# A graph-network kernel: where the fused node pieces stand in the last attention groups

## The reference, cut to what matters

```python
ft = (hn @ W_att).reshape(n, H, DH)            # H = 10 heads of DH = 13: 130 numbers a node
scores = einsum('ehd,ehd->eh', ft[src], ft[dst]) / sqrt(DH)
ex = exp(scores - segment_max(scores, dst)[dst])
a = ex / segment_sum(ex, dst)[dst]
agg = segment_sum(ft[src] * a[:, :, None], dst)
out = elu(agg).reshape(n, H * DH) @ hr_w + hr_b + hn
out = layer_norm(out); skip2 = out
out = elu(elu(out @ w1 + b1) @ w2 + b2) + skip2
x = x + out; h = relu(layer_norm(x))           # the second block's input
```

## Time and profile before

| | |
|---|---|
| median of 3 runs | 3837.37 us (3832.4 to 3840.59) |
| the profiled execution | 3839.02 us, its span 3837.3 us |
| TensorE busy | 3360.4 us (88%) |
| VectorE busy | 2355.0 us (61%) |
| ScalarE busy | 1781.7 us (46%) |
| GpSimd busy | 2447.0 us (64%) |
| mean granted clock of TensorE | 0.889 of full speed |

### The profile page before, as it was taken

One profiled execution on the slowest core, in us unless ns is written; L12 is line 12 of the kernel. 1 busy time (PEld: TensorE's weight loads), 2 busy tenths in 40 slices (PEclk: granted clock), 3 DMA queues, 4 the chain that ended last, 5 costly groups with the idle time before them and its releaser, 6 DMA issues. The chain is left out here.

```text
span 3837.3 us, 59210 instructions
## 1 busy us (share of the span) xinstructions
PE 3360.4 (88%) x20346; PEld 2104.3 (55%) x20346; DVE 2355.0 (61%) x3511; ACT 1781.7 (46%) x4855; POOL 2447.0 (64%) x2604
## 2 busy tenths in 40 slices
PE   5788888888888888888878487999999999999999
PEld 4566666666666666666655354444444444445444
DVE  8798888888888888888655375222422242224222
ACT  4787887878888888788543255000200020002000
POOL 2577777777777777777765000777277737764775
PEclk7688888888888888888888698999999999999999
DMA  6433333334333333334322514888788868887886
GB/s 205 127 105 107 107 104 106 103 107 108 103 107 104 107 107 104 107 103 128 89 56 50 109 36 128 256 256 257 218 256 256 256 211 254 253 246 219 262 262 189
DMA packets 493480, 600.98 MB, mean 157 GB/s; under 512 B 61561, under 2 KB 424420, under 8 KB 492910
## 3 DMA queue, kind: packets, MB, share of 16 engines
q1 hardware_dynamic: 355270, 337.43, 29.2%
q0 software_dynamic: 82960, 172.57, 18.2%
q10 hardware_dynamic: 54968, 87.43, 6.4%
HBM read 489.80 MB, written 109.00 MB: 156 GB/s over the span
## 5 line engine op out<-in xcount | busy, mean ns | idle before, releaser
L984 POOL DMA_INDIRECT fts<-ft_tab,src_all x1568 | 1480.7, 944 | 504.2 <-issue 473.4
L2668 PE MATMUL cv_acc<-cv_cnt,cv_parts 128*128 128x512 bf16 x5880 | 1271.9, 379 | 0.0
L2668 PEld LDWEIGHTS cv_acc<-cv_cnt,cv_parts 128*128 128x128 bf16 x5880 | 575.3, 98 | 690.8
L2419 POOL DMA_INDIRECT cv_slots<-hs_tab,slot_idx x640 | 605.0, 945 | 195.0 <-issue 195.0
L1016 DVE TENSOR_TENSOR ohk<-iota_ps,key_cols 128x784 bf16<-128x784 f32 x704 | 651.3, 967 | 5.5
L1432 PE MATMUL agg_ps<-terms,oh 128*64 128x141 f32 x2744 | 566.4, 382 | 82.8 <-DVE terms L1053 82.2
L1432 PEld LDWEIGHTS agg_ps<-terms,oh 128*64 128x64 f32 x2744 | 492.0, 192 | 131.3 <-DVE terms L1053 116.4
L1193 ACT ACTIVATE dist_l<-lo_iota,low 128x128 bf16<-128x128 f16 x1760 | 533.1, 387 | 16.5 <-ACT low L1188 0.4
L1372 PE MATMUL adj_ps<-ohk,ohl 128*128 128x196 bf16 x2816 | 379.4, 262 | 93.5 <-ACT strip L1245 48.0
L1245 ACT CAST strip<-adj_ps 128x392 bf16<-128x392 f32 x704 | 334.2, 475 | 238.8 <-PE adj_ps L1375 205.0
L1030 DVE TENSOR_TENSOR prod<-ftd_ps,fts 128x780 f32<-128x780 f32 (+1 forms) x392 | 271.1, 691 | 242.0 <-DMA fts<-ft_tab,src_all 208.4
(11 more groups left out here) (345 smaller groups left out, 3455.0 us busy)
## 6 DMA issues: line engine op xcount, KB each, us to landing
cv_cnt<-adj SPq DMA_DIRECT2D x88, 2048.0 KB, 8.3
cv_cnt<-adj SPq DMA_DIRECT2D x44, 2176.0 KB
adj<-strip ACTq DMA_DIRECT2D x176, 392.0 KB
fts<-ft_tab,src_all POOLq DMA_INDIRECT x1568
win<-ft_tab SPq DMA_DIRECT2D x196, 65.0 KB
hs_tab<-cv_hs ACTq DMA_DIRECT2D x24, 448.0 KB, 3.6
cv_slots<-hs_tab,slot_idx POOLq DMA_INDIRECT x640
agg_tab<-res SPq DMA_DIRECT2D x196, 35.2 KB
```

Source lines behind the costliest of these rows:

```text
L984: nc.gpsimd.indirect_dma_start(fts[u][:, k, :], None, ft_tab[:, :], bass.IndirectOffsetOnAxis(src_all[:, n, k:k + 1], 0)).then_inc(gathere ...
L2419: nc.gpsimd.indirect_dma_start(slots[n % RING][:, e, :], None, hs_tab[:, :], bass.IndirectOffsetOnAxis(rows_at, 0)).then_inc(slots_in[n % ...
L2668: last = nc.tensor.matmul(a[:, 0:width], parts[:, r, b, :], cnt[q][:, 0:width // SUB, (b - b0) * SUB:(b - b0 + 1) * SUB], start=(b == 0 an ...
```

## The change

Five things change, in `attention` alone. `STARTS` goes from (0, 5, 17, 22) to (0, 5, 15, 20), and `SLOTS_AT` from 177 to 176: units 0 and 1 begin one group earlier, units 2 and 3 two groups earlier. GpSimd's wait for `shift_done` stands in counted groups only. VectorE puts weighted and fade_boundary at the start of a step without counts. ScalarE puts `res` ahead of the first half's pieces. TensorE has an order of its own for steps without counts: nearness, first half's pieces, closeness, the sums, last_features, the last sum, first_features, second half's pieces. No instruction is added or taken away on the three compute engines.

```diff
--- before.py
+++ after.py
@@ -86,7 +86,7 @@
 FT = FB * BATCH
 UNITS = ((0, 4), (4, 4), (8, 3), (11, 3))
 UW = 4
-STARTS = (0, 5, 17, 22)
+STARTS = (0, 5, 15, 20)
 PHASES = 17
 FINAL_AT = 130
 CQ = ((0, 393), (393, 392), (785, 392), (1177, 392))
@@ -782,7 +782,7 @@
     x_sb, eps, hnT_dram, hT_tab = (g[k] for k in ("x_sb", "eps", "hnT_dram", "hT_tab"))
     R3 = HD + 1 - P
     WEIGHTS_AT = 2 * UN
-    SLOTS_AT = NSD + 1
+    SLOTS_AT = NSD
     NODES_AT = NSD - 8
     LD = 6
     FU = 6
@@ -978,7 +978,7 @@
                 if n >= FU:
                     pool.wait_ge(terms_done, n - FU + 1)
                 for k in range(GC):
-                    if k == HC and n >= LAG + 1:
+                    if k == HC and LAG + 1 <= n < NSD:
 
                         pool.wait_ge(shift_done, n - LAG)
                     nc.gpsimd.indirect_dma_start(fts[u][:, k, :], None, ft_tab[:, :],
@@ -1153,23 +1153,27 @@
 
             def body(k):
                 one, two, late = k.at(-1), k.at(-2), k.at(-LAG)
+                def weights():
+                    weighted(late)
+                    if late.after(1):
+                        fade_boundary(late)
                 if k.counted():
                     low_one_hots(k)
                     key_one_hots(k, 0)
                     key_one_hots(k, 1)
                     key_one_hots(k, 2)
+                elif late.exists():
+                    weights()
                 if one.exists():
                     first_products(one)
                 if two.exists():
                     highest(two)
                 if k.counted():
                     key_one_hots(k, 3)
+                    if late.exists():
+                        weights()
                 for unit, phase in units_at(k, 0):
                     nodes(unit, phase)
-                if late.exists():
-                    weighted(late)
-                    if late.after(1):
-                        fade_boundary(late)
                 if one.exists():
                     last_products(one)
                 for unit, phase in units_at(k, 1):
@@ -1329,12 +1333,12 @@
                     numerators(late)
                 if nxt.exists():
                     destination_rows(nxt)
-                for unit, phase in units_at(k, 0):
-                    nodes(unit, phase)
                 if k.counted():
                     copy_quarter(k, 1)
                 if over.exists():
                     result(over)
+                for unit, phase in units_at(k, 0):
+                    nodes(unit, phase)
                 if nxt.exists():
                     destination_columns(nxt)
                 for unit, phase in units_at(k, 1):
@@ -1530,32 +1534,49 @@
                     broadcast_highest(late)
                 if two.exists():
                     turn_highest(two)
-                for unit, phase in units_at(k, 0):
-                    nodes(unit, phase)
-                if k.counted():
-                    count(k, 0)
-                if nxt.exists():
-                    nearness(nxt)
-                if k.counted():
-                    count(k, 1)
-                    count(k, 2)
-                if one.exists():
-                    last_features(one)
-                if nxt.exists():
-                    closeness(nxt)
-                for unit, phase in units_at(k, 1):
-                    nodes(unit, phase)
-                if k.counted():
-                    count(k, 3)
-                if late.exists():
-                    first_sums(late)
-                    later_sums(late)
-                if k.exists():
-                    first_features(k)
-                if late.exists():
+                def last_sums():
                     if late.after(1):
                         carried(late)
                     last_sum(late)
+
+                def counted():
+                    count(k, 0)
+                    if nxt.exists():
+                        nearness(nxt)
+                    count(k, 1)
+                    count(k, 2)
+                    if one.exists():
+                        last_features(one)
+                    if nxt.exists():
+                        closeness(nxt)
+                    count(k, 3)
+                    if late.exists():
+                        first_sums(late)
+                        later_sums(late)
+                    first_features(k)
+                    if late.exists():
+                        last_sums()
+
+                def uncounted():
+                    if nxt.exists():
+                        nearness(nxt)
+                    for unit, phase in units_at(k, 0):
+                        nodes(unit, phase)
+                    if nxt.exists():
+                        closeness(nxt)
+                    first_sums(late)
+                    later_sums(late)
+                    if one.exists():
+                        last_features(one)
+                    last_sums()
+                    if k.exists():
+                        first_features(k)
+                    for unit, phase in units_at(k, 1):
+                        nodes(unit, phase)
+                if k.counted():
+                    counted()
+                else:
+                    uncounted()
             zero = Group(0)
             nearness(zero)
             closeness(zero)
```

## The result

The changed kernel takes 3801.81 us (median of 4 runs, 3794.61 to 3807.49), the kernel before 3836.02 us beside it. The ratio is 0.9909, with a 95% interval from 0.9885 to 0.9933: 34 us faster (26 to 44). The profiled execution of the changed kernel took 3796.92 us; it is one of the two quick ones of the four.

What follows compares the result with a forecast made beforehand. Gathers were taken to bound the counted steps, then TensorE's work plus waits. Gains of 16 (waits), 3 (earlier units), 2 (clock) and 0 (GpSimd) made 21 us: 3837.4 to 3816.4 us, own range 3808 to 3825, eight in ten 3802 to 3833.

Steps and rivals of the forecast that it cites:

- TensorE's clock: Steps 179 to 194: granted clock rises from 0.82 to 0.84 as waits shrink, worth 3 us, taken as 2.
- What bounds the kernel: Attention stage: GpSimd's gathers at 9.99 us a group up to 1905 us, then TensorE's work plus waits between its pieces.
- GpSimd's wait: Groups 176 to 195: removing 29.5 us of shift waits gains 0, since GpSimd is ahead of the other engines.
- The waits of TensorE: Steps 179 to 194: the new order cuts TensorE's 40.0 us of waits to 24 us, 16 us won.
- eight crossings: Second half's piece to the next step's first: TensorE waits 1.0 us for the elu each time, 8 us in all.
- The entry for the other waits: Smaller TensorE waits in steps 179 to 194, 14.1 us before, put at 11 us after.
- Units a group sooner: Earlier slots move work into steps 176 to 178, where gathers set the pace: 3 us won, bounds 0 and 7.1.
- The rule of the Trainium skill: TensorE's slow clock is the default and activity releases it; a denser order would give back up to 27 us.
- the first: Steps from 176: 28 us of waits won, 8 us from the clock, 3 from earlier starts; 39 us, 3798 us; chance 0.14.
- Rival 2: Waits only change place: first_features waits for `prod` in every step, 6 us won, clock unchanged, 3831 us; chance 0.16.
- Rival 3: Slower: sums wait for weighting behind the previous step's second-half pieces on VectorE; 54 us of waits, 3848 us; chance 0.10.

Runs made afterwards that it cites:

- fillers: Two unread 128x512 products behind nearness in each of 17 steps, and closeness behind last_features, in the changed kernel: 3791.3 us, 0.9882; without these products 0.993.
- e3: New orders of TensorE, VectorE and ScalarE alone in the kernel before, with old unit starts and shift wait: 3804.1 us, 0.9921.
- e4: GpSimd's shift wait put back in all groups of the changed kernel: 3805.9 us, 0.9926 against the kernel before.
- closeness early: Closeness moved directly behind nearness in steps without counts, in the changed kernel: 3821.6 us, 0.9964 against the kernel before.
- the changed kernel's second profile: The changed kernel measured once more, unedited, nothing changed: 3802.9 us, 0.9912 against the kernel before.

## Why the prediction was right and where it was wrong

The forecast was 3816.4 us, 21 us faster, with a range down to 3802; measured were 3801.8 us, 34 us faster, just outside. Its direction holds, its size does not. The step that failed is the term of TensorE's clock, put at 2 us.

- *What bounds the kernel*: right. Counted steps are unchanged, and the steps from 176 are bound by TensorE's work and the waits between its pieces.
- *GpSimd's wait*, taken as 0: right. Without it the kernel before takes 1.0001 of its time, and part of the wait moves to the buffer, as said. In the changed kernel that wait is 0.6 us only.
- *The waits of TensorE*, taken as 16 us: 16.7 us came in steps 176 to 198 (in steps 179 to 194 from 40.0 to 27.3 us, of which a part is the step's worth of pieces that left the stretch). That the sum fits so well is partly luck, since errors cancel in it. Closeness kept 8.6 us where 0 was said, mostly behind table loads; the sums have 1.7 us where 5 were said; `up` and `down` wait 6.3 us for the elu in seven places, about 1 us each, where eight crossings of 1 us were said; and `ftd_ps` waits 4.6 us for `prod`, which had no entry of its own. (The entry for the other waits adds up to 10.4 us and was put down as 11.)
- *Units a group sooner*, taken as 3 us: 5 us alone (1.5 to 9), within what can be told. What they are worth on top of the new orders was not resolved.
- *TensorE's clock*, taken as 2 us: this is the term that failed. In the profiled executions it is 23.8 us over steps 176 to 198; in steps 179 to 194, for which it was reckoned, busy time fell from 165.1 to 142.3 us, 22.9 us, of which some 3 or 4 us (an estimate, by 20 of 922 products) are pieces that left the stretch. It was mis-sized twice. First the rise: the step of the reckoning was that a busy share like that of the counted steps gives their clock, 0.84. TensorE is now busy for 142.3 of 169.6 us, 84%, the counted steps have 85%, and yet the clock is 0.90: a rise of eight hundredths and not of two. The closeness experiment shows the same from the other side: a like sum of waits gave 0.80 or 0.90. Second, and less, the price: all of the slow time in these 16 steps was put at 27 us from one burst. Over the eleven profiles without fillers the busy time of steps 176 to 198 goes from 223.6 us at 0.73 to 182.0 us at 0.90, about 2.4 us for each hundredth. The 16 steps have four fifths of that busy time, so from 0.82 to 1.0 it would be about 35 us (an estimate; no profile here is above 0.90). How great the term is in a typical execution is less sure: the profiles of e3 and e4 give it 19.8 and 14.3 us.
- *The rule of the Trainium skill*: the page TensorE: Matmul & The Clock Gate ("What's actually happening") has activity release the slow state. That was the reading that I set aside for the counted steps' 0.84. The fillers' 21 us and the 0.90 of the denser order agree with it. It does not by itself order all the profiles here: TensorE is busy for 84% of the stretch with closeness early, at 0.80, and for 82% in the changed kernel's second profile, at 0.90.
- *The rivals*: the nearest was the first, 3798 us with a chance of 0.14, with 28 us of waits and 8 us of clock; it came with 17 and 24. Rival 2 (first_features wait for `prod` in every step) did not come. When VectorE's order is changed alone a wait for `prod` of 33.0 us appears, but it is that of last_features for the first products: the first half of the rival's mechanism, at another place. Rival 3 (slower) did not come with the whole change; its side of the result is what half of the change gives.
- *The traces against the medians*: the profiled execution of the changed kernel lies 5 us below its median and that of the kernel before 3 us above, so the span is 42 us shorter in the traces and the time 34 us in the medians.

## What to carry to other kernels

Price the clock of TensorE like a term of its own before you count it as small: take busy time and granted clock of the stretch from more than one execution. A wait that comes back in each step can cost more than its length, as closeness early did. Compare clocks over several executions before you give a difference to an order. Two engines' orders that meet in a chain are to be moved together: here each alone lost time, 20 and 38 us, and both won 30. When a wait can't be removed, a product that nobody reads, put where TensorE would pause, is worth a try.

## What the runs showed of the hardware that I had not expected

With the sum of the waits nearly the same, 39.1 and 39.9 us, the granted clock of the stretch was 0.90 in one order and 0.80 in another, whose times do not meet. What makes a wait cost clock was not settled: the kernels differ in the number of long waits and in how regularly they come, and no run here holds one of these fixed while it changes the other. Part of such a difference is the execution and not the order: with nearly the same waits (37.7 and 37.9 us, of the same kinds) the clock was 0.89 or 0.85, and TensorE was busy for 16.4 of 17.0 us at 0.52 in a stretch where another execution had 1.00. Further, unread work made a kernel faster: 34 added products, 21 us less. And between executions of the changed kernel the clock over the span moved by three to five thousandths and the time by 13 to 14 us with it, which widens its intervals.
